# Convolution tiles emitted inside the normalisation loop, eight tiles behind it, in a fused S4 plus int4 feed-forward kernel

## The chip, the cores and the metric

The kernel runs on all 8 cores of one Trainium2 chip. The 16384 rows of the input are split over the cores, 2048 rows each; the cores exchange nothing. The metric is the device time in microseconds of the slowest core.

## The reference

```python
xn = _layernorm(x, axis=-1)                       # x: (2, 8192, 4096) f32, over 4096 channels
# S4: K is a 4096-long kernel made from the small parameters, by Cauchy sums and an inverse FFT
y  = irfft(rfft(xn, n=2 * L) * rfft(K, n=2 * L), n=2 * L)[..., :L] + D[0] * xn   # causal convolution
gate, up = xn @ dequant(gate_q), xn @ dequant(up_q)      # int4 weights, groups of 128, 4096 x 11008
ffn = (silu(gate) * up) @ dequant(down_q)                # 11008 x 4096
x   = x + y + ffn
```

The convolution runs along the last axis (L = 4096), so every row of x is convolved with K by itself.

## The kernel before, in words

The kernel is written with raw engine queues: every `@block.<engine>` function appends instructions to the in-order program of one engine, and semaphores order the engines among each other. What comes first in the Python text comes first in that engine's queue. There are five stages.

1. Set-up (lines 182 to 522). Scales and zeros of the int4 weights are rewritten in DRAM as bf16, the S4 kernel K is worked out, and the Toeplitz tile `s_T` (128 partitions x 4096 bf16) is filled by 128 small DMAs from GpSimd's queue, with K shifted by one more place in each row.
2. Normalisation and transposition (lines 540 to 621), for 16 row tiles `mt` of 128 rows. SyncE's queue loads `s_x` (128 x 4096 f32, 2 MB, two buffers); before load `mt` it waits for the normalisation of tile `mt-2`. VectorE takes `bn_stats` over 8 pieces and `bn_aggr`; ScalarE takes the square root (line 572), VectorE makes the bias, ScalarE writes the normalised bf16 tile `s_xnb` (line 591), TensorE transposes it in two rounds of 16 blocks into PSUM `ptr_ps` (one buffer, line 607), and ScalarE copies each round to `s_xnT` (line 618), which holds all 2048 rows with the channels on partitions.
3. Convolution (lines 623 to 665), again for 16 row tiles. For each half of 2048 output columns TensorE runs matmuls of `s_xnT` blocks against `s_T` into PSUM `pcv` (one buffer of 2048 f32, line 643): 40 matmuls in the first half, 104 in the second. ScalarE copies `pcv` to `s_cv` (one buffer, line 657), and SyncE's queue writes `s_cv` to the DRAM scratch `cscr` (line 663, 1 MB each). The next half's first matmul waits for the copy; the next copy waits for the write.
4. Stage A (lines 703 to 861): 86 tiles of 128 intermediate channels: dequantisation on VectorE, gate and up matmuls, silu, product, spill to DRAM. Its first loads wait for the last copy of the convolution (`cs_p1`).
5. Stage B (lines 896 on): the down projection in 8 column blocks, with the sum of all branches.

The convolution of tile `mt` needs only the transposed tile `mt` (`marks[(mt, 1)]`) and `s_T`. The change touches the order of stages 2 and 3 and nothing in stages 1, 4 and 5.

Of the kernel before, what the change touches and what calls it, by code (L numbers as in the profile page):

```python
# [17 lines left out]
MROWS = ROWS // NCORE  # L18
NMT = MROWS // 128
# [50 lines left out]
def build():  # L70
# [17 lines left out]
    out = nc.dram_tensor("out", [MROWS, DM], F32, kind="ExternalOutput").ap()  # L88
# [10 lines left out]
    cscr = nc.dram_tensor("cscr", [MROWS, DM], F32, kind="Internal").ap()  # L99
# [14 lines left out]
    CVS = Sem(mk0(nc.semaphore("CVS")))  # L114
# [3 lines left out]
    TB = Sem(mk0(nc.semaphore("TB")))  # L118
    CV = Sem(mk0(nc.semaphore("CV")))
    CS = Sem(mk0(nc.semaphore("CS")))  # L120
    CT = Sem(mk0(nc.semaphore("CT")))
# [8 lines left out]
    s_xnT = es_xnT.enter_context(nc.sbuf_tensor("s_xnT", [128, KT * MROWS], BF16))  # L130

    es_T = ExitStack()
    s_T = es_T.enter_context(nc.sbuf_tensor("s_T", [128, 32 * 128], BF16))

    marks = {}

    with es0, nc.Block() as block:
# [44 lines left out]
        @block.sync  # L182
        def _(sync):
            for dst, src in [
                (s_lam[:], lam), (s_p[:], p_ri), (s_q[:], q_ri),
                (s_vc[:], vc.rearrange("m k c -> m (k c)")),
                (s_ct[:], ct_in.rearrange("o n c -> (o n) c")),
                (s_bp[:], bp), (s_lsr[:], lsr), (s_dd[:], dd_in),
                (s_cr[:], cr_pc), (s_ci[:], ci_pc),
                (s_CosM[:], CosM), (s_SinM[:], SinM), (s_SinMneg[:], SinMneg),  # L190
                (s_Wtr[:], Wtr), (s_Wti[:], Wti),
                (s_Er[:], Er), (s_Ei[:], Ei), (s_Eineg[:], Eineg),
                (s_id[:], ident),
            ]:
                LD.inc(sync.dma_start(out=dst, in_=src), 16)
# [326 lines left out]
        ds_T = TB.n  # L522
# [9 lines left out]
        s_cv = mkp1(nc.sbuf_tensor("s_cv", [128, 2048], F32))  # L532

        ptr_ps = mkp1(nc.psum_tensor("ptr_ps", [128, 2048], BF16))
        pcv = mkp1(nc.psum_tensor("pcv", [128, 2048], F32))

        xl_mark = [0] * NMT
        xn_mark = [0] * NMT

        for mt in range(NMT):  # L540
            @block.sync
# [78 lines left out]
                        in_=ptr_ps[:].rearrange("p (K c) -> p K c", c=128)))  # L620
                marks[(mt, rnd)] = CS.n

        for mt in range(NMT):
            for half in range(2):
                @block.tensor
                def _(tensor):
                    tensor.wait_ge(CS.h, marks[(mt, 1)])
                    if mt == 0 and half == 0:
                        tensor.wait_ge(TB.h, ds_T)
                    ckey = ("cv", mt, half - 1) if half else ("cv", mt - 1, 1)  # L630
                    if ckey in marks:
                        tensor.wait_ge(CS.h, marks[ckey])
                    ilo_h = 16 * half
                    args = []
                    for j_blk in range(ilo_h + 16):
                        for bl in range(4):
                            i_lo = max(ilo_h + 4 * bl, j_blk)
                            i_hi = ilo_h + 4 * bl + 4
                            if i_lo < i_hi:
                                args.append((j_blk, i_lo, i_hi))  # L640
                    for idx, (j_blk, i_lo, i_hi) in enumerate(args):
                        d_lo = i_lo - j_blk
                        mm = tensor.matmul(  # L643
                            out=pcv[:, (i_lo - ilo_h) * 128:(i_hi - ilo_h) * 128],
                            lhsT=s_xnT[:, MROWS * j_blk + 128 * mt: MROWS * j_blk + 128 * (mt + 1)],
                            rhs=s_T[:, 128 * d_lo:128 * (d_lo + (i_hi - i_lo))],
                            start=(j_blk == 0), stop=(j_blk == i_hi - 1))
                        if idx == len(args) - 1:
                            CT.inc(mm)
                marks[("cvt", mt, half)] = CT.n  # L650

                @block.scalar
                def _(scalar):
                    scalar.wait_ge(CT.h, marks[("cvt", mt, half)])
                    if mt or half:
                        scalar.wait_ge(CVS.h, CVS.n)
                    CS.inc(scalar.copy(out=s_cv[:], in_=pcv[:]))  # L657
                marks[("cv", mt, half)] = CS.n

                @block.sync  # L660
                def _(sync):
                    sync.wait_ge(CS.h, marks[("cv", mt, half)])
                    CVS.inc(sync.dma_start(
                        out=cscr[128 * mt:128 * (mt + 1), 2048 * half:2048 * (half + 1)],
                        in_=s_cv[:]), 16)

        cs_p1 = CS.n
        cvs_conv = CVS.n
# [417 lines left out]
def _get_nc():  # L1086
    if "nc" not in _BUILD_CACHE:
        _BUILD_CACHE["nc"] = build()
    return _BUILD_CACHE["nc"]
# [36 lines left out]
```

## Time and profile before

| what | us |
|---|---|
| median of the timed runs (10522.64 to 10533.34, 2 runs) | 10527.99 |
| the profiled execution | 9118.58 |
| its span on the slowest core (core 1; the others 9065.1 to 9105.8) | 9117.0 |
| of it, normalisation stage, from the first `bn_stats` to the first matmul of the convolution | 288.6 to 577.4 |
| of it, convolution stage, to the last matmul | 577.4 to 1202.1 |
| stage A, first gate matmul | 1253.3 |

The span is the time from the first to the last instruction of the slowest core in one profiled execution. TensorE is busy for 85% of it. The profiled execution is shorter than the timed runs; durations in this document come from the profiled one. In its rows, PE is TensorE's matmuls, PEld its weight loads, DVE VectorE, ACT ScalarE, SPq the DMA issues of SyncE's queue.

### The profile page before, as it was taken

Reading aid. Unit: us, or ns where it says so; the run is one execution under the profiler, and the core shown is the slowest. Engines: PE = TensorE matmul, PEld = TensorE weight load, DVE = VectorE, ACT = ScalarE, POOL = GpSimd, SP = SyncE. Lnnn points to the kernel's source line nnn. Section 1 sums busy time; section 2 is a strip of 40 time slices with the busy share of each in tenths; the row PEclk is TensorE's granted clock in tenths of the full one; section 3 lists DMA queues with packets and bytes.
Section 4 is the critical chain, followed back from the end, with each engine's and each line's share of the span. In section 5 each row is a group of like instructions: output and inputs, shape, how many; then the busy total and the mean of one; then the engine's idle time right before and its main releaser. Section 6 shows DMA issues by size and latency. Waiting matters only on the chain.

```text
span 9117.0 us, 89069 instructions; the slowest of 8 cores (9065.1 to 9117.0 us)
## 1 busy us (share of the span) xinstructions
PE 7761.9 (85%) x35892; PEld 3527.7 (39%) x35892; DVE 2730.5 (30%) x5716; ACT 602.5 (7%) x394; POOL 276.8 (3%) x516
## 2 busy tenths in 40 slices
PE   1158879999999999999999999949687696876969
PEld 0123334444444444444444444424233242332424
DVE  4210023333333333333333333331423414234131
ACT  0541100000000000000000000000000000000000
POOL 0200000000000000000000000000000000000000
PEclk9998989999999999999999999979898898988989
DMA  1311155554444444444455555445766756667574
GB/s 41 112 69 56 51 91 96 101 94 93 95 94 97 96 99 99 93 93 95 94 96 94 100 98 95 91 159 192 231 214 213 246 185 235 210 218 245 187 228 168
DMA packets 1179348, 1199.89 MB, mean 132 GB/s; under 512 B 854906, under 2 KB 903430, under 8 KB 1110854
## 3 DMA queue, kind: packets, MB, share of 16 engines
q1 hardware_dynamic: 945978, 731.65, 28.0%
q10 hardware_dynamic: 198144, 360.80, 19.1%
q0 software_dynamic: 34816, 101.74, 3.3%
q8 instruction: 285, 4.67, 0.2%
q14 instruction: 125, 1.02, 0.0%
HBM read 1077.43 MB, written 116.56 MB: 131 GB/s over the span
## 4 chain that ended last, share of the span: by engine, by line
PE 83%; DMA 7%; DVE 4%; ACT 3%; SPq 1%; issue 1%; DVEq 0%; ACTq 0%; POOL 0%; POOLq 0%
PE pg L799 26%; PE pu L811 26%; PE pd L1012 24%; PE pcv L643 6%; DMA rpz<-zsc_d 4%; DVE s_nib L944 1%; DVE wd_slab L947 1%; DVE s_nib L937 1%; ACT s_xnb L591 1%; PE ptr_ps L607 1%; ACT s_cv L657 1%; ACT s_xnT L618 1%; DMA hbl<-hscr 1%; SPq L920 0%; ACT L657 0%
## 5 line engine op out<-in xcount | busy, mean ns | idle before, releaser
L1012 PE MATMUL pd<-wd_slab,hbl 128*128 128x512 bf16 x11008 | 2396.7, 381 | 691.8 <-DMA hbl<-hscr 323.5
L799 PE MATMUL pg<-s_xnT,wg 128*128 128x512 bf16 x11008 | 2392.6, 379 | 51.2 <-DVE wg L771 51.2
L811 PE MATMUL pu<-s_xnT,wu 128*128 128x512 bf16 x11008 | 2389.9, 379 | 0.0
L1012 PEld LDWEIGHTS pd<-wd_slab,hbl 128*128 128x128 bf16 x11008 | 1081.3, 98 | 2007.2 <-issue 721.6
L799 PEld LDWEIGHTS pg<-s_xnT,wg 128*128 128x128 bf16 x11008 | 1076.4, 98 | 1353.1 <-issue 55.0
L811 PEld LDWEIGHTS pu<-s_xnT,wu 128*128 128x128 bf16 x11008 | 1078.4, 98 | 1297.6
L762 DVE TENSOR_SCALAR s_nib<-ig 128x256 int16<-128x256 int16 x1376 | 237.2, 278 | 2775.6 <-DMA rep_zg<-zsc_g 2059.7
L643 PE MATMUL pcv<-s_T,s_xnT 128*128 128x512 bf16 (+3 forms) x2304 | 518.1, 391 | 106.6 <-ACT s_cv L657 106.6
L1034 DVE TENSOR_SCALAR xnc<-xcb,s_rstd,s_nbias 128x512 f32<-128x512 f32 x128 | 69.9, 546 | 1660.1 <-PE pd L1012 1516.0
L825 ACT ACT_TABLE_LOAD x86 | 110.3, 1283 | 4505.5 <-PE pg L799 4505.5
L643 PEld LDWEIGHTS pcv<-s_T,s_xnT 128*128 128x128 bf16 x2304 | 233.5, 104 | 391.1 <-issue 186.9
L833 DVE TENSOR_TENSOR hb<-hb,pu 128x2048 bf16<-128x2048 bf16 x86 | 196.7, 2287 | 617.1 <-PE pu L811 617.1
L762 DVE TENSOR_SCALAR s_nib<-iu 128x256 int16<-128x256 int16 x1376 | 237.4, 278 | 285.9 <-DMA rep_zu<-zsc_u 227.3
L937 DVE TENSOR_SCALAR s_nib<-id4b 128x1024 int16<-128x1024 int16 (+1 forms) x352 | 172.0, 614 | 493.2 <-DMA rpz<-zsc_d 439.8
L607 PE MATMUL ptr_ps<-s_idbf,s_xnb 128*128 128x128 bf16 x512 | 59.7, 310 | 241.5 <-ACT s_xnb L591 187.0
L768 DVE TENSOR_TENSOR s_tmpb<-s_nib,rep_zu 128x1024 bf16<-128x1024 int16 x344 | 238.1, 692 | 35.8
L768 DVE TENSOR_TENSOR s_tmpb<-s_nib,rep_zg 128x1024 bf16<-128x1024 int16 x344 | 238.1, 692 | 35.8
L771 DVE TENSOR_TENSOR wg<-s_tmpb,rep_sg 128x1024 bf16<-128x1024 bf16 x344 | 238.1, 692 | 35.7
L771 DVE TENSOR_TENSOR wu<-s_tmpb,rep_su 128x1024 bf16<-128x1024 bf16 x344 | 238.1, 692 | 35.7
L967 POOL DMA_DIRECT2D xcb<-x x128 | 68.8, 538 | 5677.2 <-issue 5677.2
L944 DVE TENSOR_TENSOR s_nib<-s_nib,rpz 128x4096 bf16<-128x4096 int16 (+1 forms) x88 | 197.4, 2244 | 10.2 <-DVE s_nib L937 1.4
L947 DVE TENSOR_TENSOR wd_slab<-s_nib,rps 128x4096 bf16<-128x4096 bf16 (+1 forms) x88 | 197.4, 2243 | 9.1
(123 smaller groups left out, 1281.5 us busy)
## 6 DMA issues: line engine op xcount, KB each, us to landing
hbl<-hscr SPq DMA_DIRECT2D x320, 1024.0 KB, 6.6
rep_sg<-ssc_g ACTq DMA_DIRECT2D x344, 256.0 KB, 6.9
rep_zg<-zsc_g ACTq DMA_DIRECT2D x344, 256.0 KB, 8.2
rep_su<-ssc_u ACTq DMA_DIRECT2D x344, 256.0 KB, 6.7
rep_zu<-zsc_u ACTq DMA_DIRECT2D x344, 256.0 KB, 8.5
rps<-ssc_d SPq DMA_DIRECT2D x80, 1024.0 KB, 7.9
rpz<-zsc_d SPq DMA_DIRECT2D x80, 1024.0 KB, 10.2
hscr<-hb SPq DMA_DIRECT2D x86, 512.0 KB, 9.4
```

The lines of the kernel that those rows point to most:

```text
L607: mm = tensor.transpose(out=ptr_ps[:, 128 * ft16:128 * (ft16 + 1)], in_=s_xnb[mt % 2][:, 128 * ft:128 * (ft + 1)], identity=s_idbf[:])
L643: mm = tensor.matmul(out=pcv[:, (i_lo - ilo_h) * 128:(i_hi - ilo_h) * 128], lhsT=s_xnT[:, MROWS * j_blk + 128 * mt: MROWS * j_blk + 128 * ...
L762: CV.inc(vector.tensor_scalar(out=nv[:, 0:8, :, 2 * sh:2 * sh + 2], in0=iv[:, 8 * q:8 * (q + 1), :, :], scalar1=(4 * sh), scalar2=15, op0= ...
L768: CV.inc(vector.tensor_tensor(out=s_tmpb[:], in0=s_nib[:], in1=reps[("z", mat, q % 3)][:], op=ALU.subtract))
L771: CV.inc(vector.tensor_tensor(out=wbuf[:, 1024 * q:1024 * (q + 1)], in0=s_tmpb[:], in1=reps[("s", mat, q % 3)][:], op=ALU.mult))
L799: mm = tensor.matmul(out=pg[:, 512 * c:512 * (c + 1)], lhsT=wg[t % 2][:, 128 * K:128 * (K + 1)], rhs=s_xnT[:, MROWS * K + 512 * c: MROWS * ...
L811: mm = tensor.matmul(out=pu[:, 512 * c:512 * (c + 1)], lhsT=wu[t % 2][:, 128 * K:128 * (K + 1)], rhs=s_xnT[:, MROWS * K + 512 * c: MROWS * ...
L833: CV.inc(vector.tensor_tensor(out=hb[t % 2][:], in0=hb[t % 2][:], in1=pu[:], op=ALU.mult))
L937: CV.inc(vector.tensor_scalar(out=nv[:, 0:bw, :, 2 * sh:2 * sh + 2], in0=iv[:, 0:bw, :, :], scalar1=(4 * sh), scalar2=15, op0=ALU.logical_ ...
L944: CV.inc(vector.tensor_tensor(out=tb2[:, 0:bw * 512], in0=s_nib2[:, 0:bw * 512], in1=rpz[b % 2][:, 0:bw * 512], op=ALU.subtract))
L947: CV.inc(vector.tensor_tensor(out=wd_slab[:, 512 * i0:512 * (i0 + bw)], in0=tb2[:, 0:bw * 512], in1=rps[b % 2][:, 0:bw * 512], op=ALU.mult))
L1012: mm = tensor.matmul(out=pd[pbase + jj][:], lhsT=hbl[hB % NHBUF][:, 512 * (i - i0h) + 128 * jj: 512 * (i - i0h) + 128 * (jj + 1)], rhs=wd_ ...
```

## The change

The body of the convolution loop becomes a function `emit_conv(mt)`, defined ahead of the normalisation loop. Normalisation iteration `mt` with `mt >= 8` ends with a call of `emit_conv(mt - 8)`, and after the loop tiles 8 to 15 follow. The instructions themselves, their buffers and the waits that they carry stay as they were; only the places in each engine's queue differ. `NMT` is 16.

```diff
+        emit_conv_holder = [None]
+
+        def emit_conv(mt):
             for half in range(2):
                 @block.tensor
                 def _(tensor):
...
+        emit_conv_holder[0] = emit_conv
+
+
+        for mt in range(NMT):
+            @block.sync
+            def _(sync):
...
+                XQp[mt % 2].inc(sync.dma_start(out=s_x[mt % 2][:], in_=x_in[128 * mt:128 * (mt + 1), :]), 16)
...
+                marks[(mt, rnd)] = CS.n
+
+            if mt >= 8:
+                emit_conv_holder[0](mt - 8)
+
+        for mt_c in range(NMT - 8, NMT):
+            emit_conv_holder[0](mt_c)
```

The rows below are the engines' queues in order; "waits" names the semaphores of a row (CS is counted by ScalarE, CV by VectorE, CT by TensorE, CVS by the writes to `cscr`, XQ by the loads of `s_x`). Line numbers are those of each kernel's own file.

SyncE's queue before, at the end of the 16 loads of `s_x`:

```order
L548 DMA s_x<-x 128x4096 [waits CS]
L541 UNCONDITIONAL_BRANCH
L548 DMA s_x<-x 128x4096 [waits CS]
L660 UNCONDITIONAL_BRANCH
L663 DMA cscr<-s_cv 128x2048 [waits CS]
L660 UNCONDITIONAL_BRANCH
L663 DMA cscr<-s_cv 128x2048 [waits CS]
```

All loads stand ahead of the first write. SyncE's queue now, from the load of tile 8 to that of tile 9:

```order
L597 DMA s_x<-x 128x4096 [waits CS]
L578 UNCONDITIONAL_BRANCH
L581 DMA cscr<-s_cv 128x2048 [waits CS]
L578 UNCONDITIONAL_BRANCH
L581 DMA cscr<-s_cv 128x2048 [waits CS]
L590 UNCONDITIONAL_BRANCH
L597 DMA s_x<-x 128x4096 [waits CS]
```

The load of tile 9 now stands behind both writes of convolution tile 0, and so on to the load of tile 15 behind those of tile 6.

TensorE's queue before, inside the transposes (the normalised tile `s_xnb` against the identity `s_idbf`):

```order
L607 MATMUL ptr_ps<-s_idbf,s_xnb 128x128 x15
L597 UNCONDITIONAL_BRANCH
L607 MATMUL ptr_ps<-s_idbf,s_xnb 128x128 [waits CS]
L607 MATMUL ptr_ps<-s_idbf,s_xnb 128x128 x15
L597 UNCONDITIONAL_BRANCH
```

And now, from the end of convolution tile 0 through the transposes of tile 9 to the start of convolution tile 1:

```order
L561 MATMUL pcv<-s_T,s_xnT 128x128
L646 UNCONDITIONAL_BRANCH
L656 MATMUL ptr_ps<-s_idbf,s_xnb 128x128 [waits CS]
L656 MATMUL ptr_ps<-s_idbf,s_xnb 128x128 x15
L646 UNCONDITIONAL_BRANCH
L656 MATMUL ptr_ps<-s_idbf,s_xnb 128x128 [waits CS]
L656 MATMUL ptr_ps<-s_idbf,s_xnb 128x128 x15
L543 UNCONDITIONAL_BRANCH
L561 MATMUL pcv<-s_T,s_xnT 128x512 [waits CS]
```

Seven times (tiles 9 to 15) a convolution tile now stands behind the transposes of a later row tile on TensorE. ScalarE's queue now, in the same place:

```order
L575 COPY s_cv<-pcv 128x2048 [waits CT]
L570 UNCONDITIONAL_BRANCH
L575 COPY s_cv<-pcv 128x2048 [waits CT,CVS]
L618 UNCONDITIONAL_BRANCH
L621 ACTIVATE s_rstd<-s_v 128x1 [waits CV]
L635 UNCONDITIONAL_BRANCH
L640 ACTIVATE s_xnb<-s_x,s_nbias,s_rstd 128x4096 [waits CV,CT]
```

The square root and the normalisation of tile 9 stand behind both copies of convolution tile 0.

## Rows read from the trace of the kernel before

**Rows 1.** The page: its head and part 1 for TensorE.
```profile
span 9117.0 us, 89069 instructions; the slowest of 8 cores (9065.1 to 9117.0 us)
...
PE 7761.9 (85%) x35892; PEld 3527.7 (39%) x35892; DVE 2730.5 (30%) x5716; ACT 602.5 (7%) x394; POOL 276.8 (3%) x516
```

**Rows 2.** Windows: stretch, its length, busy time (count) by engine, clock, DMA, GB/s.
```profile
290.00:577.40 287.40, 59.44 (x512) 52.11 (x513) 92.12 (x206) 202.73 (x126) 51.94 (x110) 1.00 0.32 109
577.40:1205.40 628.00, 518.13 (x2307) 233.40 (x2304) 0.00 (x0) 103.91 (x66) 0.00 (x0) 0.89 0.13 52
...
1500.00:2000.00 500.00, 500.00 (x2319) 226.62 (x2317) 170.04 (x441) 28.44 (x18) 0.00 (x0) 1.00 0.53 95
```

**Rows 3.** Timeline of one normalisation tile: start us, length us, engine, line, operation.
```profile
437.61 1.28 ACT L572 ACT_TABLE_LOAD   x1
438.90 0.20 ACT L572 ACTIVATE s_rstd<-s_v 128x1 f32<-128x1 f32 x1
...
439.76 1.28 ACT L591 ACT_TABLE_LOAD   x1 [0.65 <-DVE s_nbias L581]
441.05 3.80 ACT L591 ACTIVATE s_xnb<-s_x,s_nbias,s_rstd 128x4096 bf16<-128x4096 f32 x1
444.96 4.84 DVE L557 BATCH_NORM_STATS2 s_st<-s_x 128x6 f32<-128x512 f32 x8 [5.33 <-ACT s_xnb L591]
...
445.11 1.86 PE L607 MATMUL ptr_ps<-s_idbf,s_xnb 128*128 128x128 bf16 x16 [10.76 <-ACT s_xnb L591]
...
450.36 1.87 PE L607 MATMUL ptr_ps<-s_idbf,s_xnb 128*128 128x128 bf16 x16 [3.38 <-ACT s_xnT L618]
...
450.64 0.16 DVE L565 RECIPROCAL s_v<-s_v 128x1 f32<-128x1 f32 x1
...
458.93 3.80 ACT L591 ACTIVATE s_xnb<-s_x,s_nbias,s_rstd 128x4096 bf16<-128x4096 f32 x1
```

**Rows 4.** Timeline of the convolution's first tiles and its last matmuls.
```profile
575.78 1.87 PE L607 MATMUL ptr_ps<-s_idbf,s_xnb 128*128 128x128 bf16 x16 [3.38 <-ACT s_xnT L618]
...
577.45 8.56 PE L643 MATMUL pcv<-s_T,s_xnT 128*128 128x512 bf16 x40
...
589.39 23.01 PE L643 MATMUL pcv<-s_T,s_xnT 128*128 128x512 bf16 x104 [3.38 <-ACT s_cv L657]
...
615.85 9.20 PE L643 MATMUL pcv<-s_T,s_xnT 128*128 128x512 bf16 x40 [3.44 <-ACT s_cv L657]
...
628.49 24.12 PE L643 MATMUL pcv<-s_T,s_xnT 128*128 128x512 bf16 x104 [3.44 <-ACT s_cv L657]
...
652.74 1.28 ACT L657 ACT_TABLE_LOAD   x1 [24.40 <-PE pcv L643]
654.03 1.87 ACT L657 COPY s_cv<-pcv 128x2048 f32<-128x2048 f32 x1
...
656.04 10.18 PE L643 MATMUL pcv<-s_T,s_xnT 128*128 128x512 bf16 x40 [3.44 <-ACT s_cv L657]
...
669.66 24.01 PE L643 MATMUL pcv<-s_T,s_xnT 128*128 128x512 bf16 x104 [3.44 <-ACT s_cv L657]
...
1194.81 7.30 PE L643 MATMUL pcv<-s_T,s_xnT 128*128 128x512 bf16 x39
```

**Rows 5.** Waits in the stretch 580 to 1205 (us in total, times, longest).
```profile
PE pcv L643 <- ACT s_cv L657: 106.6, 31, 3.4
```

**Rows 6.** The line of the loads of `s_x` (16 of them), and their landing.
```profile
L548 SPq DMA_DIRECT2D s_x<-x x16: 327/328/429, 279.4 to 534.6; - x16
...
DMA to landing us min/median/max: 7.6/8.0/15.4
```

**Rows 7.** DMA issues in the stretch 600 to 1200: count, KB each, median us to landing.
```profile
cscr<-s_cv SPq DMA_DIRECT2D x30, 1024.0 KB, 3.9
```

**Rows 8.** Timeline, SyncE's queue: the last write of the convolution and the issue behind it.
```profile
1205.48 0.32 SPq L663 DMA_DIRECT2D cscr<-s_cv  x1
1205.89 0.39 SPq L713 DMA_DIRECT2D ig<-gqw  x1
```

More of the change, by code:

```diff
@@ L538, in build, with _ @@
         xn_mark = [0] * NMT
+        emit_conv_holder = [None]
+        def emit_conv(mt):
+            for half in range(2):
+                @block.tensor
+                def _(tensor):
+                    tensor.wait_ge(CS.h, marks[(mt, 1)])
+                    if mt == 0 and half == 0:
+                        tensor.wait_ge(TB.h, ds_T)
+                    ckey = ("cv", mt, half - 1) if half else ("cv", mt - 1, 1)
+                    if ckey in marks:
+                        tensor.wait_ge(CS.h, marks[ckey])
+                    ilo_h = 16 * half
+                    args = []
+                    for j_blk in range(ilo_h + 16):
+                        for bl in range(4):
+                            i_lo = max(ilo_h + 4 * bl, j_blk)
+                            i_hi = ilo_h + 4 * bl + 4
+                            if i_lo < i_hi:
+                                args.append((j_blk, i_lo, i_hi))
+                    for idx, (j_blk, i_lo, i_hi) in enumerate(args):
+                        d_lo = i_lo - j_blk
+                        mm = tensor.matmul(
+                            out=pcv[:, (i_lo - ilo_h) * 128:(i_hi - ilo_h) * 128],
+                            lhsT=s_xnT[:, MROWS * j_blk + 128 * mt: MROWS * j_blk + 128 * (mt + 1)],
+                            rhs=s_T[:, 128 * d_lo:128 * (d_lo + (i_hi - i_lo))],
+                            start=(j_blk == 0), stop=(j_blk == i_hi - 1))
+                        if idx == len(args) - 1:
+                            CT.inc(mm)
+                marks[("cvt", mt, half)] = CT.n
+                @block.scalar
+                def _(scalar):
+                    scalar.wait_ge(CT.h, marks[("cvt", mt, half)])
+                    if mt or half:
+                        scalar.wait_ge(CVS.h, CVS.n)
+                    CS.inc(scalar.copy(out=s_cv[:], in_=pcv[:]))
+                marks[("cv", mt, half)] = CS.n
+                @block.sync
+                def _(sync):
+                    sync.wait_ge(CS.h, marks[("cv", mt, half)])
+                    CVS.inc(sync.dma_start(
+                        out=cscr[128 * mt:128 * (mt + 1), 2048 * half:2048 * (half + 1)],
+                        in_=s_cv[:]), 16)
+        emit_conv_holder[0] = emit_conv
         for mt in range(NMT):
@@ L621, in build @@
                 marks[(mt, rnd)] = CS.n
[L623 to L665, printed above, removed]
+            if mt >= 8:
+                emit_conv_holder[0](mt - 8)
+        for mt_c in range(NMT - 8, NMT):
+            emit_conv_holder[0](mt_c)
         cs_p1 = CS.n
```

## The prediction

> **What bounds the kernel now.** I read the page first: TensorE is busy for 85% of a span of 9117.0 us [rows 1], so a stage's time is mostly a question of what TensorE does there. The change touches only the two stages between 290 and 1205 us, so the second view was the windows. In the normalisation stage ScalarE is busy 202.73 of 287.40 us and TensorE only 59.44; in the convolution stage TensorE is busy 518.13 of 628.00 us, ScalarE 103.91 and VectorE 0 [rows 2]. The two stages look as if they could lie on top of each other. The timeline then says what a tile costs in each.
>
> A normalisation tile takes 458.93 - 441.05 = 17.88 us [rows 3], and ScalarE sets it: square root, normalisation and the two copies follow one another on it, while VectorE's statistics of the next tile run beside the copies (444.96 to 450.80) and the load of `s_x` (8.0 us to landing [rows 6]) was issued a tile ahead. A convolution tile takes (1202.11 - 577.45 + 3.44) / 16 = 39.25 us [rows 4]: 144 matmuls, and twice 3.4 us in which TensorE waits for the copy of `pcv`, 106.6 us in 31 waits [rows 5]. So 7 normalisation tiles and 16 convolution tiles, which is what the change reorders, cost 7 x 17.88 + 624.7 = 749.8 us.
>
> **The change, part by part.** No instruction, buffer or wait is added or removed; what moves is the place in three in-order queues. Up to the transposes of row tile 8 nothing differs. `s_T` was filled long before that (TensorE's wait for it, TB, stands on convolution tile 0 now as before, and the first matmul of the convolution follows the last transposes without a gap [rows 4]). From there the new order is: convolution 0, row tile 9, convolution 1, row tile 10, ..., row tile 15, convolution 7, and then convolution 8 to 15 as before.
>
> Could row tile 9 run beside convolution 0? Three queues say no.
> - TensorE: the transposes of tile 9 stand between convolution 0 and convolution 1, so whatever they wait for holds up convolution 1.
> - ScalarE: the square root and normalisation of tile 9 stand behind both copies of convolution 0, the second of which waits for the last matmul of convolution 0.
> - SyncE's queue: the load of tile 9 stands behind both writes of convolution 0, and the second write waits for that same copy. Before, this load was issued a tile ahead; now it is not issued until convolution 0 has ended. VectorE's statistics wait for it. This is the costliest part of the move.
>
> So between two convolution tiles the whole chain of one row tile stands exposed, and longer than before, since the load and the statistics no longer lie beside anything. The hole, from the last matmul of convolution `mt-9` to the first of convolution `mt-8`:
> - copy of `pcv`: from the last matmul's end, 628.49 + 24.12 = 652.61, to 654.03 + 1.87 = 655.90, 3.3 us [rows 4];
> - the write's issue, and the load's 0.41 us behind it [rows 8], 0.5 us with the semaphore;
> - the load of 2 MB. Alone it lands in 8.0 us [rows 6]. Here a write of 1 MB (3.9 us to landing [rows 7]) was issued on the same queue 0.41 us before it. If the two share nothing the load takes 8.0 us, if it goes wholly behind the write 3.9 + 8.0 - 0.4 = 11.5 us. The longest load in the trace, 15.4 us, about twice 7.6 [rows 6], fits two loads of 2 MB issued together at the start of the stage, the second behind the first; it is the nearest row, so I take 11.5 us. Bounds 8.0 and 15.4;
> - statistics to reciprocal: 444.96 to 450.80, 5.8 us [rows 3];
> - square root's table load to the end of the normalisation: 437.61 to 444.85, 7.2 us, with 0.2 us from VectorE ahead of it [rows 3];
> - transposes, the first copy of `ptr_ps` and the second round of transposes: 445.11 to 452.0, 6.9 us, with 0.3 us ahead [rows 3]. The second copy (its table load included, 3.2 us) does lie beside the next convolution; it is the one part of ScalarE's work that the interleaving hides.
> Sum: 3.3 + 0.5 + 11.5 + 5.8 + 7.4 + 7.2 = 35.7 us.
>
> The convolution between two holes, first matmul to last: the three tiles shown take 35.0 us (577.45 to 612.40), 36.8 us and 37.6 us [rows 4]. The differences are TensorE's clock: the granted clock over the stage is 0.89, against 1.00 in stage A, where 2319 matmuls fit in 500 us, 215.6 ns each at 2.4 GHz [rows 2]. After each wait of 3.4 us part of the matmuls run at 1.2 GHz. In the new order every interleaved convolution starts directly behind a round of transposes, as the first one of before did, so its row is the nearest: 35.5 us, between 35.0 and 37.6.
>
> A rule of the Trainium skill bears on this: "TensorE: Matmul & The Clock Gate", section "HAM oscillation — how this bites in real kernels", says that a TensorE which pauses between bursts has its clock taken back to half and starts each burst slowly. It speaks against interleaving, since the change adds seven long pauses. The trace agrees for short pauses already (0.89 above), and because the old order pauses before every half anyway, the rule adds nothing to the sum beyond the 35.0 to 37.6 us.
>
> The sum: convolution 0, 35.5; seven times 35.7 + 35.5 = 71.2, 498.4; convolution 8 to 15, 8 x 39.25 = 314.0. Together 847.9 us against 749.8, so +98 us. Seen per tile: 71.2 against 17.88 + 39.25 = 57.1, +14.1 us, seven times, of which 12 us are the load and 6 us the statistics, less the hidden copy and one wait of 3.4 us. Stage A still starts from the last copy of convolution 15, so all of it is on the path. The profiled execution would go from 9118.6 to 9217 us.
>
> The median of the timed runs, 10528 us, is 1409 us above the profiled execution, and no row says why. The hole is made of DMA, VectorE and ScalarE time but for two rounds of transposes (3.7 us), so I carry the difference over unscaled: 10528 + 98 = 10626 us, +0.9%. A measurement of this kernel tells about 2% from no change, so this counts as the same.
>
> **Rivals.**
>
> (a) The overlap happens: normalisation lies beside the convolution and disappears. For it: the windows, ScalarE idle for five sixths of the convolution stage and VectorE for all of it. Then 7 x 17.88 = 125 us go, 10403 us. It decides at one place: whether the load of tile 9 can be issued, and the square root started, before the last matmul of convolution 0. The order of the queues says no. If only the load were early, the hole would be 35.7 - 12.0 - 5.8 = 17.9 us, the whole 35.5 + 7 x 53.4 + 314.0 = 723.3 against 749.8, and the result 10501 us, still faster than before. Chance 3%, both together.
>
> (b) TensorE rests half of the time and the convolution runs faster. In the rows a tile has 144 matmuls of 67584 columns in all, 28.2 us at 2.4 GHz, and one inner wait of 3.4, 31.6 us; against 35.5 that is 8 x 3.9 = 31 us back, 10595 us. Against it: before each half the engine has still been idle for 3.4 us. Chance 10%.
>
> (c) A stronger form of (b), for the timed runs alone. By a rule of the Trainium skill ("TensorE: Matmul & The Clock Gate", section "Wait — 56ns, not 53.3ns?"), dense matmuls on three or more cores of a die bring its clock down to 13/16. No row here shows that; it would make an estimate of 49.8 ns more for each of some 35000 matmuls, 1.1 ms for stage A alone, so it could be what separates 10528 from 9118. As a mechanism of this kernel, priced from the rows: if all matmuls of the timed runs take 10528 / 9118 as long, 28.2 us become 32.6, and pauses that lift this for the 8 interleaved tiles give 8 x 4.4 = 35 us back on 98, 10591 us. Chance 10%.
>
> (d) The load lands later still: all eight cores now write 1 MB and load 2 MB at the same moments, and it takes the 15.4 us of the longest row, with the convolution at 37.6 us. Then +98 + 7 x 3.9 + 8 x 2.1 = 142, 10670 us. Chance 12%.
>
> **How the numbers follow.** The forecast of 10626 has 63%; (a) 3%, (b) 10%, (c) 10%, (d) 12%, and 2% for something that I don't see. The bounds of the load alone give -25 and +27 us, those of the convolution -4 and +17. The range reaches over (b), (c) and (d): 10570 to 10680. Slower by over 2% would need 30 us more in each of seven holes, or a disturbance elsewhere, 3%; faster by over 2% needs more than all of (a), 1%; within 2%, 96%.
>
> **What would show it.** In the profile after, the line of the `s_x` loads issues at most once per some 71 us from tile 9 on, with a landing of 11 to 12 us; TensorE waits for `s_xnb` about 28 us seven times; VectorE's `bn_stats` waits for a DMA and not for ScalarE; stage A's first gate matmul comes near 1253 + 98 = 1351 us, and from there on all is as before. I am wrong if the loads of tiles 9 to 15 are issued inside a convolution tile, if they land in 8 us (then +73), or if the stages behind 1351 us change length.

## The result, and the profile after

| | before | after |
|---|---|---|
| median of the runs, us | 9957.72 (9105.18 to 10547.51, 11 runs) | 9185.51 (9166.82 to 10524.6, 12 runs) |
| ratio after to before | | 1.0077, 95% interval 1.0058 to 1.0095 |
| profiled execution, us | 9118.58 | 9176.61 |
| granted clock, mean of the span | 0.950 to 0.953 | 0.943 to 0.944 |

The change makes the kernel 0.8% slower. In some executions of either kernel the cores of one die, a group of four of the eight cores, have a lower granted clock (down to 0.81) and take up to 10547 us, so the two medians cannot be compared; the ratio leaves such executions out, and every time given below is that of the slowest core of a die without this, as the median over a series, beside the same number of the kernel before in the same series. The granted clock is the share of full speed (2.4 GHz) that TensorE is given.

The page after (core 6 is its slowest core), head, part 1 and two groups of part 5:

```profile
span 9175.1 us, 89069 instructions; the slowest of 8 cores (9138.2 to 9175.1 us)
...
PE 7749.1 (84%) x35892; PEld 3525.1 (38%) x35892; DVE 2730.6 (30%) x5716; ACT 602.5 (7%) x394; POOL 276.8 (3%) x516
...
L561 PE MATMUL pcv<-s_T,s_xnT 128*128 128x512 bf16 (+3 forms) x2304 | 508.5, 386 | 82.8 <-ACT s_cv L575 82.8
...
L656 PE MATMUL ptr_ps<-s_idbf,s_xnb 128*128 128x128 bf16 x512 | 59.7, 310 | 356.3 <-ACT s_xnb L640 302.1
```

The same instructions and nearly the same busy times as in [rows 1] (TensorE 7749.1 us for 7761.9); what has grown is idle time. The waits of TensorE, VectorE and ScalarE in the stretch 460 to 1260 us (total, times, longest):

```profile
DVE s_st L606 <- DMA s_x<-x: 424.5, 7, 61.4
...
PE ptr_ps L656 <- ACT s_xnb L640: 188.4, 7, 28.1
...
ACT L621 <- DVE s_v L614: 112.8, 7, 17.3
PE pcv L561 <- ACT s_cv L575: 82.8, 24, 3.7
```

Seven times VectorE's statistics wait for a load, ScalarE's square root waits for the statistics, and TensorE waits 27 us for the normalised tile. The wait for the copy of `pcv` [rows 5] happens 24 times in place of 31: seven of them have become part of the long ones. The timeline of one period, which answers to [rows 3] and [rows 4]:

```profile
537.75 23.01 PE L561 MATMUL pcv<-s_T,s_xnT 128*128 128x512 bf16 x104 [3.72 <-ACT s_cv L575]
560.89 1.28 ACT L575 ACT_TABLE_LOAD   x1 [23.29 <-PE pcv L561]
562.19 1.86 ACT L575 COPY s_cv<-pcv 128x2048 f32<-128x2048 f32 x1
564.53 0.38 SPq L597 DMA_DIRECT2D s_x<-x  x1
573.96 4.84 DVE L606 BATCH_NORM_STATS2 s_st<-s_x 128x6 f32<-128x512 f32 x8 [61.37 <-DMA s_x<-x]
...
579.64 0.16 DVE L614 RECIPROCAL s_v<-s_v 128x1 f32<-128x1 f32 x1
579.88 1.28 ACT L621 ACT_TABLE_LOAD   x1 [15.83 <-DVE s_v L614]
...
583.33 3.80 ACT L640 ACTIVATE s_xnb<-s_x,s_nbias,s_rstd 128x4096 bf16<-128x4096 f32 x1
587.39 1.87 PE L656 MATMUL ptr_ps<-s_idbf,s_xnb 128*128 128x128 bf16 x16 [26.63 <-ACT s_xnb L640]
...
592.64 1.86 PE L656 MATMUL ptr_ps<-s_idbf,s_xnb 128*128 128x128 bf16 x16 [3.38 <-ACT s_xnT L667]
594.30 8.53 PE L561 MATMUL pcv<-s_T,s_xnT 128*128 128x512 bf16 x40
```

Read downwards it is one chain with nothing beside it. The last matmul ends at 537.75 + 23.01 = 560.76 and the next convolution begins at 594.30: a hole of 33.5 us. This load is issued at 564.53 and the statistics begin at 573.96, 9.4 us later; every other part of the hole has the length that the prediction gave it, within 0.1 us. The line of the loads has landings of

```profile
L597 SPq DMA_DIRECT2D s_x<-x x16: 327/350/432, 281.2 to 906.4; - x16
...
DMA to landing us min/median/max: 8.1/9.3/17.2
```

and the last load is issued at 906.4 us, where it was issued at 534.6 [rows 6]. From the first matmul of the convolution to the last it is now 824.9 to 828.6 us on the eight cores. Before, the 16 convolution tiles took 620.5 to 626.3 us, and 7 normalisation tiles another 125.2. By the medians the reordering costs 826.6 - (624.5 + 125.2) = 77 us in these two stages, 75 to 82 us on single cores. The ratio says 53 to 86 us for the whole kernel, so the stages account for it.

The profiled executions differ by less, 58 us, since two other stretches differ from core to core by as much as 10 us and more. The time from the last convolution matmul to the first gate matmul of stage A is 38 to 41 us on all cores after, and before it was 40 to 41 us on four and 51 to 53 us on the other four, the slowest core among them; in later runs of other orders it is 38 to 51 us with the same code. From the first gate matmul to the end it was 7825 to 7864 us before and is 7821 to 7853 us after. What causes this scatter stays open; no run here shows it to be an effect of the change.

### The profile page after: what moved, and what is told of

The parts are those of the page before. It is cut to its first block, busy times and chain, and to the rows that moved or that the text cites. A ratio compares the mean times of both kernels' runs of the same rounds, so it can differ in the third digit from the quotient of the medians.

```text
span 9175.1 us, 89069 instructions; the slowest of 8 cores (9138.2 to 9175.1 us)
## 1 busy us (share of the span) xinstructions
PE 7749.1 (84%) x35892; PEld 3525.1 (38%) x35892; DVE 2730.6 (30%) x5716; ACT 602.5 (7%) x394; POOL 276.8 (3%) x516
## 4 chain that ended last, share of the span: by engine, by line
PE 82%; DMA 8%; DVE 5%; ACT 3%; SPq 1%; issue 1%; DVEq 0%; ACTq 0%; POOL 0%; POOLq 0%
PE pg L810 26%; PE pu L822 26%; PE pd L1023 24%; PE pcv L561 6%; DMA rpz<-zsc_d 4%; DVE s_nib L955 1%; DVE wd_slab L958 1%; DVE s_nib L948 1%; DMA s_x<-x 1%; ACT s_xnb L640 1%; PE ptr_ps L656 1%; ACT s_cv L575 1%; DMA hbl<-hscr 1%; SPq L931 1%; ACT s_xnT L667 0%
## 5 line engine op out<-in xcount | busy, mean ns | idle before, releaser
L844 DVE TENSOR_TENSOR hb<-hb,pu 128x2048 bf16<-128x2048 bf16 x86 | 196.7, 2287 | 935.2 <-PE pu L822 935.2
L779 DVE TENSOR_TENSOR s_tmpb<-s_nib,rep_zu 128x1024 bf16<-128x1024 int16 x344 | 238.1, 692 | 35.8
L782 DVE TENSOR_TENSOR wu<-s_tmpb,rep_su 128x1024 bf16<-128x1024 bf16 x344 | 238.1, 692 | 35.7
L779 DVE TENSOR_TENSOR s_tmpb<-s_nib,rep_zg 128x1024 bf16<-128x1024 int16 x344 | 238.1, 692 | 35.8
L782 DVE TENSOR_TENSOR wg<-s_tmpb,rep_sg 128x1024 bf16<-128x1024 bf16 x344 | 238.1, 692 | 35.7
L606 DVE BATCH_NORM_STATS2 s_st<-s_x 128x6 f32<-128x512 f32 x128 | 77.5, 678 | 479.1 <-DMA s_x<-x 436.5
```

The costliest lines, as they stand in the source:

```text
L779: CV.inc(vector.tensor_tensor(out=s_tmpb[:], in0=s_nib[:], in1=reps[("z", mat, q % 3)][:], op=ALU.subtract))
L782: CV.inc(vector.tensor_tensor(out=wbuf[:, 1024 * q:1024 * (q + 1)], in0=s_tmpb[:], in1=reps[("s", mat, q % 3)][:], op=ALU.mult))
L844: CV.inc(vector.tensor_tensor(out=hb[t % 2][:], in0=hb[t % 2][:], in1=pu[:], op=ALU.mult))
```

## The experiments

All kernels here split the normalisation into `ln_load`, `ln_stats` (statistics and square root), `ln_norm` and `ln_tr(mt, round)`, and the convolution into `conv_half(mt, half)`, each with the code of before, so that an order can be written in a few lines. "..." marks lines left out.

**The load early.**

```diff
...
+        ln_load(0)
         for mt in range(NMT):
-            ln_load(mt)
+            if mt + 1 < NMT:
+                ln_load(mt + 1)
             ln_stats(mt)
...
```

> The changed kernel, with one move: the load of row tile mt+1 is emitted ahead of convolution tile mt-8 in SyncE's queue, nothing else. Theory A (the load behind the writes is the costliest part of the hole, and VectorE's statistics come with it): the hole between two interleaved convolution tiles falls from 33.6 us to 33.6 - 0.5 - 9.4 - 5.9 = 17.8 us, the period from 68.2 to 52.4, the last convolution matmul comes 7 x 15.8 = 111 us earlier than in the changed kernel, and the kernel is 0.3 to 0.5% faster than before. Theory B (ScalarE's order, square root and normalisation behind both copies, sets the hole, the load would be late anyway): hole stays above 30 us, time as the changed kernel's, ratio to before about 1.008.

Measured: 9048 us (9035 to 9059) against 9077 of before (9068 to 9091), 0.3% faster. The timeline (core 7, whose matmuls ran at a lower clock in this execution; the hole has hardly any matmuls in it, and on core 3, at the usual clock, it is 17.7 us too):

```profile
467.82 28.06 PE L643 MATMUL pcv<-s_T,s_xnT 128*128 128x512 bf16 x104 [3.38 <-ACT s_cv L657]
506.69 1.87 PE L608 MATMUL ptr_ps<-s_idbf,s_xnb 128*128 128x128 bf16 x16 [10.82 <-ACT s_xnb L592]
511.94 1.87 PE L608 MATMUL ptr_ps<-s_idbf,s_xnb 128*128 128x128 bf16 x16 [3.38 <-ACT s_xnT L619]
513.60 10.74 PE L643 MATMUL pcv<-s_T,s_xnT 128*128 128x512 bf16 x40
```

The hole is 513.60 - 495.88 = 17.7 us, where 17.8 was expected. On the four cores at the usual clock the stretch from the first to the last convolution matmul takes 718 to 719 us, 108 us less than in the changed kernel (111 expected). Theory B falls: one DMA issue in the wrong place of SyncE's queue is worth 16 us of each hole (the load, and the statistics that wait for it), and without it the interleaving is already slightly better than the old order.

**Statistics and normalisation early too.** Loads two tiles ahead, and in front of each convolution tile:

```diff
...
+                if mt + 1 < NMT:
+                    ln_stats(mt + 1)
+                    ln_norm(mt + 1)
                 emit_conv(mt - 8)
```

> As the run with the early load, and also statistics, square root and normalisation of row tile mt+1 are emitted ahead of convolution tile mt-8, loads two tiles ahead. Theory A: only ScalarE's copy of pcv, a copy of ptr_ps and two rounds of transposes stay in the hole, 3.3 + 3.2 + 1.9 = 8.4 us; ScalarE delays the copy of the first half by about 2 us; period near 45 us, 7 x 7 = 50 us better than the early load alone, 0.8 to 1.0% faster than before. Theory C (TensorE's clock is what the new order costs: long pauses): the holes shrink but the convolution tiles grow from 34.6 us back to 36 or 37, which gives back up to 17 us.

Measured: 9008 us (8996 to 9009, three dies) against 9077, 0.8% faster, 40 us better than the early load alone (50 expected). The timeline of core 3, which had the usual clock here:

```profile
466.36 23.01 PE L643 MATMUL pcv<-s_T,s_xnT 128*128 128x512 bf16 x104 [4.54 <-ACT s_cv L657]
489.21 1.06 PE L608 MATMUL ptr_ps<-s_idbf,s_xnb 128*128 128x128 bf16 x16
495.99 1.87 PE L608 MATMUL ptr_ps<-s_idbf,s_xnb 128*128 128x128 bf16 x16 [5.72 <-ACT s_xnT L619]
497.65 9.02 PE L643 MATMUL pcv<-s_T,s_xnT 128*128 128x512 bf16 x40
511.68 22.62 PE L643 MATMUL pcv<-s_T,s_xnT 128*128 128x512 bf16 x104 [5.01 <-ACT s_cv L657]
```

The first round of transposes now follows the convolution at once, and the hole is 497.65 - 489.37 = 8.3 us (8.4 expected). Theory C holds in part. The tile behind this hole takes 534.30 - 497.65 = 36.7 us, and the next four 37.1 to 38.3, where the changed kernel has 34.6 to 35.8. Of some 2.2 us more on average, 1.3 are the longer wait between the halves (5.01 us, behind ScalarE's early normalisation, for 3.72); about 1 us is left for slower matmuls, some 7 us in all of the 17 that theory C allowed.

**Eleven holes in place of seven.** The changed kernel with 4 for 8 (`if mt >= 4: emit_conv(mt - 4)`).

> The changed kernel with a distance of 4 tiles in place of 8, so 11 holes in place of 7. Theory A (every hole costs the same 68.2 - 57.1 = 11.1 us against the old order): 4 x 11.1 = 44 us more than the changed kernel, ratio to before about 1.0125. Rival D (most of the changed kernel's excess is a fixed cost of mixing the stages or lies in a later stage): the ratio stays near 1.008.

Measured: 9200 us (9191 to 9203) against 9077, ratio 1.0135, and 123 us for 11 holes, 11.2 us each. The traces say the same: from the first to the last convolution matmul it is 943.8 us (median of the cores), 122.6 more than the old order takes for 16 convolution and 11 normalisation tiles (624.5 + 196.7), 11.1 us for each hole, and it was 77 / 7 = 11.0 in the changed kernel. Rival D falls: the cost goes with the number of holes.

**The load ahead of the write.** The load of the next row tile is issued between the copy of the second half and its write.

```diff
                 sync.wait_ge(CS.h, marks[("cv", mt, half)])
+                if half == 1 and mt <= 6:
+                    XQp[(mt + 9) % 2].inc(sync.dma_start(out=s_x[(mt + 9) % 2][:],
...
                 CVS.inc(sync.dma_start(
```

> The changed kernel, but the load of row tile mt+1 is issued between the copy of the second half and its write, instead of behind the write: it is as late as before, but has no write ahead of it on the queue. Theory A: the load lands in 8.0 us as in the normalisation stage, not 9.3, and issues 0.4 us earlier, so the hole falls from 33.6 to about 31.8 us, 7 x 1.8 = 13 us less than the changed kernel. If the write has nothing to do with it (eight cores loading at once), landing stays at 9.3 us.

Measured: 9160 us (9148 to 9180) against 9077, ratio 1.0091: no gain over the changed kernel's 1.0077 to be seen. The load still lands in 9.3 us, and the write behind it now takes 11.3 (one pair of core 6, near 695 us; the seven such writes of this core take 10.9 to 11.6):

```profile
s_x<-x SPq DMA_DIRECT2D x1, 2048.0 KB, 9.3
cscr<-s_cv SPq DMA_DIRECT2D x1, 1024.0 KB, 11.3
```

In the changed kernel, with the write in front, the same pair takes 4.8 us (write) and 9.3 us (load).

My expectation of 8.0 us was wrong, and the run did not tell the write from the place in the program. The next one does.

**The load alone on the queue.** The loads of tiles 9 to 15 also wait until the write has landed (`sync.wait_ge(CVS.h, CVS.n)`).

> The changed kernel, but the load of row tiles 9 to 15 also waits until the write ahead of it has landed, so that it shares the queue with nothing. If the write beside it is what makes the load land in 9.3 us and not in 8.0, it lands in 8.0 us here (the hole grows by 3.9 - 1.3 - 0.4 = about 2 us all the same); if it is that eight cores load at the same moment, or the place in the program, it stays at 9.3.

```profile
cscr<-s_cv SPq DMA_DIRECT2D x13, 1024.0 KB, 3.8
s_x<-x SPq DMA_DIRECT2D x6, 2048.0 KB, 7.6
```

These are core 2's; the eight cores' medians for the load are 7.6 to 8.4 us. That the cores load at the same moments is not what costs the rest: the load of tile 9 is issued within 9 us on all eight cores (493.0 to 502.2 us; 488.8 to 495.4 in the changed kernel), and it lands in 7.6 to 8.3 us, where it took 9.2 to 10.7. So it is the write that costs about 1.5 us, from behind as well as from in front. The hole is 35.7 us (557.77 to 593.48 on core 5), 2.2 more than 33.5, as expected. The kernel takes 9176 and 9188 us (two dies), against 9082 of before.

**The interleaving done so that it can overlap.**

```diff
...
+        for mt in range(NMT):
+            if mt + 2 < NMT:
+                ln_load(mt + 2)
+            if mt >= 3:
+                conv_half(mt - 3, 0)
+            ln_tr(mt, 0)
+            if mt + 1 < NMT:
+                ln_stats(mt + 1)
+                ln_norm(mt + 1)
+            if mt >= 3:
+                conv_half(mt - 3, 1)
+            ln_tr(mt, 1)
```

> The interleaving done so that it can overlap: convolution three tiles behind, loads two tiles ahead, statistics, square root and normalisation of row tile mt+1 emitted ahead of the copy of the second half, the first round of transposes behind the first half and the second round behind the second half, where TensorE waits for the copy of pcv anyway. Theory A (it was the order in the queues that kept the stages apart, not a shared resource): no hole but the two waits of 3.4 us per tile; the convolution starts near 355 us in place of 577 and still takes 39.3 us a tile; stage A starts some 220 us earlier than before, 2.2 to 2.5% faster than before. Theory C (the two stages get in each other's way when they really run together, on ScalarE above all: 21 us of copies, norms and table loads per tile, or in SBUF): the tile takes 42 us or more and the gain stays under 180 us.

Measured: 8813 us (8809 to 8822) against 9082 (9077 to 9116, three dies), 3.0% faster, more than I expected. One convolution tile of it and the start of the next:

```profile
392.79 9.20 PE L643 MATMUL pcv<-s_T,s_xnT 128*128 128x512 bf16 x40 [2.55 <-ACT s_cv L657]
...
401.82 1.06 PE L608 MATMUL ptr_ps<-s_idbf,s_xnb 128*128 128x128 bf16 x16
...
405.42 21.33 PE L643 MATMUL pcv<-s_T,s_xnT 128*128 128x512 bf16 x104 [2.55 <-ACT s_cv L657]
...
426.59 1.06 PE L608 MATMUL ptr_ps<-s_idbf,s_xnb 128*128 128x128 bf16 x16
...
430.19 9.20 PE L643 MATMUL pcv<-s_T,s_xnT 128*128 128x512 bf16 x40 [2.55 <-ACT s_cv L657]
```

A whole convolution tile with a whole row tile's normalisation beside it takes 430.19 - 392.79 = 37.4 us, less than the convolution alone did before (39.25 on average). The transposes lie in the waits for the copy of `pcv`, which are still 3.4 us from matmul to matmul. The granted clock of the stage (355 to 950) is 0.95 to 0.96, where it was 0.89 [rows 2]. Theory A stands, theory C falls.

**Filler in the waits.** The kernel before, in its old order, with 16 useless transposes behind each half but the last:

```diff
...
+                    for ft16 in range(16 if (mt, half) != (NMT - 1, 1) else 0):
+                        tensor.transpose(out=ptr_ps[:, 128 * ft16:128 * (ft16 + 1)],
+                                         in_=s_xnb[1][:, 128 * ft16:128 * (ft16 + 1)],
+                                         identity=s_idbf[:])
```

> The kernel before, with 16 transposes of an old tile into ptr_ps (which nothing reads any more) behind the matmuls of each half of the convolution but the last: added work that computes nothing and lies in the 3.4 us in which TensorE waits for the copy. If the pipelined kernel's shorter convolution tile (37.4 us against 39.25) comes from TensorE not standing still there, so that its clock stays up, the tile falls to about 37.4 us here too and the kernel is 16 x 1.85 = 30 us (0.3%) faster than before. If it comes from something else in the pipelined order, the tile stays at 39.25 us and the time is unchanged.

Measured: 9057 us against 9075 (medians of 6 and 10 dies; 9044.6 to 9062.4 and 9064.1 to 9094.4), 17 us less with 496 instructions more. In the traces the stage itself gives the whole 30 us: from the first to the last convolution matmul 594.6 us for 624.5 (medians of the cores). Why 17 of the 30 reach the end isn't known; the stretches behind the stage scatter by more than that, as said above. In the timeline (core 1) the tile takes 656.66 - 619.25 = 37.4 us:

```profile
619.25 7.51 PE L643 MATMUL pcv<-s_T,s_xnT 128*128 128x512 bf16 x40 [2.55 <-ACT s_cv L663]
626.60 1.06 PE L653 MATMUL ptr_ps<-s_idbf,s_xnb 128*128 128x128 bf16 x16
630.21 23.01 PE L643 MATMUL pcv<-s_T,s_xnT 128*128 128x512 bf16 x104 [2.55 <-ACT s_cv L663]
653.05 1.06 PE L653 MATMUL ptr_ps<-s_idbf,s_xnb 128*128 128x128 bf16 x16
656.66 7.51 PE L643 MATMUL pcv<-s_T,s_xnT 128*128 128x512 bf16 x40 [2.55 <-ACT s_cv L663]
```

From the second tile on it takes this every time but one (35.7). Before, 37.4 us was the better half: from the third tile on, the tiles went by turns, 41.1 us (40 matmuls in 10.18 us, 104 in 24.01, as in the last of the tiles of [rows 4]) and 37.4 us (7.5 and 23.0), 39.25 on average. TensorE pauses for 2.55 us in place of 3.44, and the clock of the stage (577 to 1180) is 0.95 to 0.96 in place of 0.89. This fits the rule of the Trainium skill that the prediction named ("TensorE: Matmul & The Clock Gate", section "HAM oscillation — how this bites in real kernels"); the trace agrees.

**The copy of `pcv` on VectorE.**

```diff
...
-                CS.inc(scalar.copy(out=s_cv[:], in_=pcv[:]))
-            marks[("cv", mt, half)] = CS.n
+                CV.inc(vector.tensor_copy(out=s_cv[:], in_=pcv[:]))
+            marks[("cv", mt, half)] = CV.n
...
```

> The pipelined kernel with pcv copied by VectorE in place of ScalarE. If the wait of 3.4 us behind each half is ScalarE's table load of 1.3 us and its copy of 1.9 us, VectorE's copy (about 2.2 us, by the product of hb and pu of the same shape, 2.3 us) makes it 2.4 us: 31 x 1.0 = 31 us less than the pipelined kernel. If VectorE's statistics stand in the way of a copy, less or nothing.

Measured: 8762 us (8754 to 8767, four dies) against 9082, and 52 us less than the pipelined kernel of the same series (31 expected). A fifth, at 8820 us with a clock of 0.86 on two of its cores in this stage, is left out; with it the median is 8766. Once more in a longer series:

> The pipelined kernel with VectorE's copy once more, in more rounds, for its ratio to before: by its undisturbed cores 9082 to 8761 us, so 0.965, between 0.960 and 0.970.

Measured: ratio 0.9652, interval 0.9619 to 0.9684. This version is faster than both kernels. Core 6:

```profile
387.85 7.51 PE L643 MATMUL pcv<-s_T,s_xnT 128*128 128x512 bf16 x40 [1.72 <-DVE s_cv L657]
395.20 1.06 PE L608 MATMUL ptr_ps<-s_idbf,s_xnb 128*128 128x128 bf16 x16
397.98 21.33 PE L643 MATMUL pcv<-s_T,s_xnT 128*128 128x512 bf16 x104 [1.72 <-DVE s_cv L657]
419.14 1.06 PE L608 MATMUL ptr_ps<-s_idbf,s_xnb 128*128 128x128 bf16 x16
421.92 7.51 PE L643 MATMUL pcv<-s_T,s_xnT 128*128 128x512 bf16 x40 [1.72 <-DVE s_cv L657]
```

The tile takes 34.1 us, 3.3 less than 37.4. Half of that are the two waits, each 0.83 us shorter; the other half is the first 40 matmuls, 7.51 us in place of 9.20. The granted clock of the stage (345 to 890) is 1.00. The pauses are shorter here and the clock doesn't fall in them; this part the 31 us expected had left out.

## Why the prediction was right and where it was wrong

- **Wrong: the step that carried the difference onto 10528 us.** The prediction put the result at 10626 us, range 10570 to 10680, and the measured median is 9185.51. The step reads "I carry the difference over unscaled: 10528 + 98"; it took two timed runs that agreed within 11 us for the level of this kernel, when the profiled execution of the same kernel stood at 9118.58 and "no row says why". Eleven runs of before have since gone from 9105 to 10547 us. The forecast on the profiled execution, 9217 us, would have been 0.4% off (9176.61). What makes such a level can be seen in the run with the early load, in the same 500 us of stage A on two cores of one chip (1500 to 2000 us; columns as in [rows 2]; first core 3, then core 7):

```profile
1500.00:2000.00 500.00, 500.00 (x2319) 226.66 (x2317) 170.02 (x441) 28.44 (x18) 0.00 (x0) 1.00 0.40 95
...
1500.00:2000.00 500.00, 500.00 (x1906) 207.15 (x1905) 140.79 (x362) 22.12 (x14) 0.00 (x0) 0.81 0.33 76
```

Both are busy with matmuls all the time; at a granted clock of 0.81 one takes 262 ns, at 1.00 it takes 216. Over the 22000 matmuls of stage A that is 1.0 ms by estimate, and there is stage B besides, so it is of the size of the 1409 us. No run here shows the clock of those two timed runs themselves.
- **Right: what the new order does.** No overlap, seven holes on the path, made of copy, load, statistics, square root, normalisation and transposes. The load is the largest part; moved alone, with the statistics behind it, it gives back the 15.8 us worked out for it (17.7 us left, 17.8 expected). Rival (a) fell with the timeline after, and its point of decision, where the load stands in SyncE's queue, was the right one.
- **Right in sign and nearly in size: the difference.** +98 us or +0.93% was forecast, +0.77% (0.58 to 0.95) was measured, and +77 us in the two stages. The period from hole to hole is about 68.3 us where 71.2 was forecast; seven times 2.9 are 20 of the 21 us between 98 and 77. The first gate matmul of stage A came at 1317 to 1324 us, not near 1351.
- **Mis-sized: the load, 11.5 us; measured 9.3.** This is 2.2 of the 2.9 us. The nearest row was badly chosen. 15.4 us for the second of two loads of 2 MB said that transfers queue up, but a write of 1 MB ahead of a load costs it only about 1.5 us: the pair is down 9.7 us after the write's issue, where the two alone take 3.8 + 7.6 = 11.4. "DMA: Bandwidth & Descriptors" of the Trainium skill, section "Two DMAs through the same engine are not ordered", says that transfers on a queue start in order but are pipelined; with the write in front the trace agrees. With the write behind the load it does so less: there the pair takes 11.7 us.
- **About right: the convolution between the holes.** 35.5 us, of a range of 35.0 to 37.6; the seven tiles behind a hole take 35.8 us (524.99 to 560.76) falling to 34.6. The three tiles of [rows 4] were too few to see that the old order goes by turns, 34.0 and 37.7 us from first matmul to last. Rival (b), a clock that recovers through the long pauses, gives some 1 us a tile at most and is no more than that. What raised the clock of the stage were filled pauses (0.95 to 0.96) and shorter ones (1.00).
- **A slip in the split per tile.** 12 us for the load and 6 for the statistics, less the hidden copy and one wait, are 11 us and not 14: the 3.3 us of the copy of `pcv`, which is part of the hole, are left out of that sentence. The sum itself has them.
- **Rivals (c) and (d).** (d) fell: no load from tile 9 on took 15 us. (c) named a clock of 13/16 as possible, and the rows above show one of 0.81; but it is there on cores 0, 1, 6 and 7, two of each die, while the other four run the same matmuls at 1.00, so it doesn't come to a whole die as (c) has it. Its mechanism, long pauses that lift this clock, fell: in the run with the load alone on the queue, core 2 has holes of about 35 us, and the 104 matmuls behind them take 26.6 to 28.1 us, as they do in the tiles without holes (27.1 to 27.2).
- **Not foreseen: the scatter of the stretches behind**, 38 to 53 us at the head of stage A alone. It is nearly as large as the forecast's error of 21 us, and its cause stays open.

## What to carry to other kernels

Where every engine runs its queue in order, moving a loop body into another loop moves all of its queues at once: ask of each DMA issue, each small ScalarE instruction and each TensorE round what now stands in front of it. Interleaving pays when the producer's loads and preparation are emitted one or two steps ahead, and the consumer's waits are filled with the producer's work; here the same idea was worth +0.8% of time in one order and -3.0% in another, -3.5% with the copy on VectorE. Let the level of a forecast come from many executions, and the difference from the timeline.

## What the runs showed of the hardware that I had not expected

- Work that computes nothing made the kernel faster (9057 us for 9075): 16 transposes in each wait of 3.4 us took the convolution tile from 39.25 us on average to 37.4, and the granted clock of the stage from 0.89 to 0.95 or 0.96.
- A write of 1 MB costs a load of 2 MB on the same queue about 1.5 us whether it is issued 0.4 us ahead of it or behind it (9.3 against 7.6 to 8.4 us). The write itself goes from 3.8 us alone to 4.8 ahead of the load and 11.3 behind it.
- In one and the same stretch of stage A two cores of a die had a granted clock of 0.81 and the other two 1.00 (262 and 216 ns for a matmul of 512 columns). In the traces kept it is always a pair of neighbouring cores: 0, 1, 6 and 7 with the early load, 4 and 5 with the filler.
